# A four-layer decoder on one core: new hand-written interleavings of two streams on every engine, and one more request for a function table

## The chip, the cores and the metric

The program runs on one core of a Trainium2 chip. Its engines are TensorE (PE in the profile; PEld is its loading of weights), VectorE (DVE), ScalarE (ACT), GpSimd (POOL) and SyncE (SP, which here only starts DMAs). Each engine runs its own list of instructions strictly in the order in which the program holds them, and waits on semaphores for the others. The metric is the device time of one execution in microseconds (us).

## The reference

Twelve sublayers run over `x` of 8 sequences x 128 tokens x 128 features; each adds its result to `x` and normalises:

```python
x = _layernorm(x + _L0_attn_ref(x, L0_attn_W_qkv, L0_attn_W_out), axis=-1)
x = _layernorm(x + _L0_xattn_ref(x, ctx_1024, ...), axis=-1)
x = _layernorm(x + _L0_ffn_ref(x, L0_ffn_gate_w, ...), axis=-1)   # 8 experts
x = _layernorm(x + _L1_attn_ref(x, ...), axis=-1)                 # linear attention, rotary
x = _layernorm(x + _L1_xattn_ref(x, ctx_1024, ...), axis=-1)
x = _layernorm(x + _L1_ffn_ref(x, ...), axis=-1)                  # 8 experts
x = _layernorm(x + _L2_attn_ref(x, ...), axis=-1)                 # kernel attention + MLP
x = _layernorm(x + _L2_xattn_ref(x, ctx_1024, ctx_1024, ...), axis=-1)
x = _layernorm(x + _L2_ffn_ref(x, ...), axis=-1)                  # 8 experts
x = _layernorm(x + _L3_attn_ref(x, ...), axis=-1)
x = _layernorm(x + _L3_xattn_ref(x, ctx_1024, ctx_1024, ...), axis=-1)
x = _layernorm(x + _L3_ffn_ref(x, ...), axis=-1)                  # quantised by max |x| of all rows
```

The gated stage that the change touches, `L3x`, needs the log of a sigmoid of its forget gate; the kernel gets it from a softplus, as Exp and then Ln on ScalarE:

```python
log_fg = jax.nn.log_sigmoid(fgate_preact[..., 0])
cs = jnp.cumsum(log_fg, axis=-1)
```

## The kernel before

The eight sequences are cut in pairs. Two pairs run at a time, as **stream a** and **stream b**, which use separate buffers and separate halves of PSUM (four banks each, used as a ring); then both streams run again for the other two pairs (two turns). A stream passes through eleven stages: L0a, L0x, L0f, L1a, L1x, L1f, L2a, L2x, L2f, L3a, L3x (the letter is a for self-attention, x for attention to the context, f for experts); a last block computes the quantised layer for all sequences.

The program of an engine is a generator for each stream. Each `yield` in it ends a **step**: a few instructions, with their waits. `take_turns` (line 402) runs the steps of the two generators in the order that `TURN_ORDER` (line 144) writes out for the engine: "a3 b1" is three steps of stream a, then one of b. Within a stream the order never changes; the table only says how the two streams interleave on that engine. Since an engine issues in order, a step of a that waits also holds back the step of b behind it, whether that one is ready or not.

The names used below, by line of the kernel:

- TensorE: `project` (L458) multiplies the attention's output by its output weights; `by_token` (L464) and `by_feature` (L470) make q, k and v; L441 transposes the normalised x; L479 transposes the maxima; L486 lays a mask or maxima into a bank; L488, L492, L507 and L510 make the scores; L525 (L834 in L1x) multiplies by values; L666 is the router's logits, L673 the experts' up and L681 their down product; L715, L719, L726, L731 and L737 belong to L1a; L843 to L1x's output.
- VectorE: L1143, L1136/L1139 and L1147 are the residual sum, its mean and variance, and the normalised x; L1177 spreads heads over a wide tile; L1192 takes the maxima of scores; L1207 divides attention by its sums; L1392 to L1407 are a chain of L1a that turns decay gates into running products.
- ScalarE: L1715/L1716 give the reciprocal root of the variance; L1743 the exponentials of the scores; L1747/L1748 the reciprocal of their sums (as the exponential of a negated log); L1808 the router's exponential; L1818 the Silu of L0f and L2f; L1877/L1878 those of L1x; L1927 the Gelu of L2a. In L3x, L1974 spreads x over four tiles, L1978/L1979 are the softplus, L1995 the decay matrices, and L2003/L2004 a reciprocal root at the end.

ScalarE must load a table before a function that the present one lacks. The kernel asks for one by name: `use(functions)` (L1680, the load itself is at L1683) records the last name and skips the load where it already holds. `exp_ln()` asks for the table with both Exp and Ln. Where the kernel doesn't ask and the table doesn't fit, the compiler puts a load of its own before the instruction; such a load is shown under the instruction's line.

Of the kernel before, what the change touches and what calls it, by code (L numbers as in the profile page):

```python
# [132 lines left out]
def group_words(g):  # L133
# [9 lines left out]

TURN_ORDER = {
# [12 lines left out]
    "dve":  # L157
# [10 lines left out]
    "act":  # L168
# [8 lines left out]
    "pool":  # L177
        "a1 b1 a1 b2 a3 b1 a1 b1 a1 b1 a3 b1 a1 b2 a1 b2 a1 b1 a4 b1 a2 b4 a1 b2 a2 b2 a1 b1 a3 b1 a1 b2 a1 b2 a1 "
        "b2 a2 b2 a1 b1 ",
    "sp":  # L180
        "a3 b6 a18 b12 a23 b26 ",
}


# [5 lines left out]
def _build(nc, ctx, dram, out):  # L190
# [24 lines left out]
    def const(name):  # L215
        a, w = CONST[name]
        return W["con_sts"][:, a:a + w]
# [24 lines left out]
    def nth(eng, name, n=1):  # L242

        counted[eng, name] = counted.get((eng, name), 0) + n
        return S(name), counted[eng, name]
# [104 lines left out]
    class Order:  # L350
# [11 lines left out]
        def link(self, ins, sem=None):  # L362
            done = self.count(ins, sem)
            self.eng.wait_ge(*done)
# [20 lines left out]
    def by_sample(ap):  # L385
        return ap.rearrange("p (u d) -> p u d", u=NS)
# [25 lines left out]
    with nc.Block(name="layers") as block:  # L412
# [1263 lines left out]
        def _(eng):  # L1676
# [3 lines left out]
            def use(functions):  # L1680

                if table[0] != functions:
                    act.preload_act_table_set(functions)  # L1683
                    table[0] = functions

            def exp_ln():
                use(EXP_LN)

            def program(g):
# [5 lines left out]
                def sem(name):  # L1695
                    return S(f"{name}_{g}")

                def told(name, n=1):
                    return nth("act", f"{name}_{g}", n)
# [4 lines left out]
                def bank(*a):  # L1704
                    act.wait_ge(*ring.full((pair, *a)))
                    return ring.bank((pair, *a))

                def free(*a):
                    return ring.free((pair, *a))
# [259 lines left out]
                def L3x():  # L1969
                    gt = s.gates  # L1970
                    exp_ln()
                    act.wait_ge(*ring.freed((pair, "L3a", "xT")))
                    for j in range(4):
                        o.count(act.activation(s.bd_c[:, :, j], by_sample(s.xT[:]), ACT.Identity,  # L1974
                                               scale=const("head16in64")[:, j:j + 1]), sem("L3x_bd") if j == 3 else None)
                    yield
                    act.wait_ge(*told("L3x_absf"))
                    link(act.activation(gt[:, 5], gt[:, 5], ACT.Exp))  # L1978
                    o.count(act.activation(gt[:, 5], gt[:, 5], ACT.Ln, bias=one[0:64]), sem("L3x_softplus"))  # L1979
                    yield  # L1980
                    yield
                    yield
                    exp_ln()
                    b = bank("L3x", "mx")
                    per_head = lambda k: b[:, 64 * k:64 * k + 64].rearrange("p (u h) -> p u h", u=NS)[:, :, 0:HC]
                    o.count(act.activation(s.small[:, :, 32:40], per_head(0), ACT.Exp, scale=-1.0))
                    link(act.copy(s.small[:, :, 40:48], per_head(1)), free("L3x", "mx"))
                    yield
                    for i in (0, 3, 1, 2):
                        exp_ln()  # L1990
                        b = bank("L3x", "D", i)
                        for j in range(4):
                            cols = slice(j * T, j * T + T)
                            h = 40 + 4 * (i % 2) + j
                            o.count(act.activation(s.p[:, i, cols], b[:, cols], ACT.Exp, bias=s.small[:, i // 2, h:h + 1]),  # L1995
                                    free("L3x", "D", i) if j == 3 else None)
                        yield
                    for u in range(NS):
                        keep("L3x", ("oT", u), s.qk[:, u])
                        yield  # L2000
                    exp_ln()
                    act.wait_ge(*told("L3x_var"))
                    link(act.activation(s.small[:, :, 48:56], s.small[:, :, 16:24], ACT.Ln, bias=eps6, scale=1.0 / DC))  # L2003
                    o.count(act.activation(s.small[:, :, 24:32], s.small[:, :, 48:56], ACT.Exp, scale=-0.5), sem("L3x_rstd"))  # L2004
                    yield
                    rstd()
                    yield
                    yield
                    yield
                    keep("L3x", "xT", xT_all[:, pair * NT:(pair + 1) * NT])  # L2010
                    yield
# [408 lines left out]
```

## Time and profile before

| | us |
|---|---|
| median of 3 runs | 1023.44 |
| lowest, highest | 1021.11, 1024.71 |
| span of the profiled execution | 1020.0 |
| TensorE busy in it | 904.2 |
| VectorE, ScalarE, GpSimd busy | 539.7, 450.7, 50.8 |

The span goes from the first to the last instruction of the core; it is 3.44 us under the median of the runs. A window or a line's row in the views gives busy time by engine, and the mean granted clock of TensorE (1.00 is full speed, 0.50 the lower one). In a timeline a row gives the start, the time from there to the end of the group, engine, line, operation, what it writes and reads, and in square brackets how long the engine had been idle before it and what released it.

### The profile page before, as it was taken

The page shows a single profiled execution, that of the slowest core. Times are in us where ns is not written, and L with a number is a line of the kernel's source. Part 1 is how long each engine was busy: PE and PEld are TensorE (multiplying, and loading weights), DVE is VectorE, ACT ScalarE, POOL GpSimd, SP SyncE. Part 2 cuts the span into 40 slices and gives each one's busy share as a digit, 9 for nine tenths or more (in the row PEclk, how much of TensorE's full clock was granted, in tenths as well). Part 3 has the DMA queues.
Part 4 walks back from the last instruction along what each step waited for, and adds up shares of the span by engine and source line. Part 5 has one row for each costly group of instructions (what it writes and reads, how often), then busy time and mean ns, then how long its engine had stood idle before and what let it go on. Part 6 is the DMA issues. An engine that isn't in the chain of part 4 may idle for free. (4 is left out here: it accounts for less than half of the span.)

```text
span 1020.0 us, 22561 instructions
## 1 busy us (share of the span) xinstructions
PE 904.2 (89%) x9368; PEld 700.2 (69%) x9368; DVE 539.7 (53%) x1569; ACT 450.7 (44%) x923; POOL 50.8 (5%) x71
## 2 busy tenths in 40 slices
PE   7689899999989998997987979989998989899772
PEld 5257768778778785666556757867887868686441
DVE  5733565653265575347636853655325547454345
ACT  2044343453454673574255233244465446433442
POOL 2300000010010000001000000001001000000000
PEclk8799989999999998999999999999999999999965
DMA  9100000401000301103000000040000030000000
GB/s 344 40 2 3 1 1 1 166 2 37 2 19 1 141 3 40 43 12 139 2 12 1 2 1 2 2 166 33 6 1 19 1 140 1 2 1 2 2 1 21
DMA packets 6838, 36.12 MB, mean 35 GB/s; under 512 B 721, under 2 KB 4305, under 8 KB 5458
## 3 DMA queue, kind: packets, MB, share of 16 engines
q1 hardware_dynamic: 6738, 34.68, 9.1%
q8 instruction: 76, 1.25, 0.5%
q14 instruction: 24, 0.20, 0.1%
HBM read 34.15 MB, written 0.52 MB: 34 GB/s over the span
## 5 line engine op out<-in xcount | busy, mean ns | idle before, releaser
L673 PE MATMUL bank<-xT,weights_F 128*128 128x256 f32 x832 | 202.9, 386 | 3.1 <-ACT p L1818 2.6
L673 PEld LDWEIGHTS bank<-xT,weights_F 128*128 128x128 f32 x832 | 152.0, 193 | 26.8 <-issue 4.2
L681 PEld LDWEIGHTS bank<-weights_F,p 128*128 128x128 f32 x1088 | 133.4, 191 | 18.8 <-DVE p L1363 7.2
L681 PE MATMUL bank<-weights_F,p 128*128 128x128 f32 x1088 | 141.3, 278 | 3.7 <-DVE p L1363 3.0
L1743 ACT ACTIVATE p<-bank 128x512 f32<-128x512 f32 x160 | 84.5, 601 | 121.0 <-PE bank L492 120.9
L1683 ACT ACT_TABLE_LOAD x76 | 97.5, 1283 | 12.9 <-DMA weights_con<-in_con 5.9
L1347 DVE SCALAR_TENSOR_TENSOR res<-bank,comb,res 128x128 f32<-128x128 f32 x184 | 55.7, 345 | 74.1 <-PE bank L681 71.6
L1184 DVE TENSOR_REDUCE m_wide<-bank 128x4 f32<-128x512 f32 x96 | 60.3, 684 | 43.4 <-PE bank L780 33.5
L1818 ACT ACTIVATE p<-bank 128x512 f32<-128x512 f32 x72 | 42.5, 597 | 91.6 <-PE bank L673 91.2
L1363 DVE TENSOR_TENSOR p<-p,bank 128x512 f32<-128x512 f32 x72 | 49.3, 685 | 47.5 <-PE bank L673 27.3
L1894 ACT ACTIVATE p<-bank 128x512 f32<-128x512 f32 x64 | 36.6, 598 | 51.3 <-PE bank L673 51.2
L492 PEld LDWEIGHTS bank<-mT,weights_con 32*128 32x128 f32 x1280 | 46.4, 194 | 17.4 <-issue 13.5
L492 PE MATMUL bank<-mT,weights_con 32*128 32x128 f32 x1280 | 55.1, 296 | 0.0
L1715 ACT ACTIVATE lnv<-mv,weights_con 128x2 f32<-128x2 f32 x56 | 16.6, 296 | 74.7 <-DVE mv L1139 72.7
L1192 DVE TENSOR_REDUCE mx<-bank 128x4 f32<-128x512 f32 x64 | 40.2, 682 | 16.5 <-PE bank L488 16.4
L2037 POOL TENSOR_TENSOR xb<-x_tok,biases 128x256 f32<-128x256 f32 x24 | 19.3, 806 | 575.1 <-DVE x_tok L1147 561.5
L525 PE MATMUL bank<-p,vz 128*32 128x128 f32 x1280 | 42.7, 280 | 4.5 <-ACT p L1743 4.4
L525 PEld LDWEIGHTS bank<-p,vz 128*32 128x32 f32 x1280 | 35.2, 112 | 11.0 <-issue 8.4
L525 PE MATMUL bank<-p,weights_con 128*32 128x128 f32 x1280 | 41.7, 275 | 0.0
L1207 DVE TENSOR_TENSOR attnT<-bank,res 128x128 f32<-128x128 f32 x32 | 9.3, 289 | 55.7 <-ACT res L1748 55.7
L525 PEld LDWEIGHTS bank<-p,weights_con 128*32 128x32 f32 x1280 | 35.9, 111 | 1.0
L1147 DVE TENSOR_SCALAR x_tok<-res,mv,rstd 128x128 f32<-128x128 f32 x88 | 26.4, 343 | 18.1 <-ACT rstd L1716 17.6
(319 smaller groups left out, 1356.0 us busy)
## 6 DMA issues: line engine op xcount, KB each, us to landing
weights_F<-in_L1f SPq DMA_DIRECT2D x2, 4096.0 KB, 13.8
weights_F<-in_L0f SPq DMA_DIRECT2D x2, 3456.0 KB, 13.4
weights_F<-in_L2f SPq DMA_DIRECT2D x2, 3456.0 KB, 12.1
weights_Y<-in_L1x_kv SPq DMA_DIRECT2D x2, 1024.0 KB, 10.6
weights_Z<-in_L1x SPq DMA_DIRECT2D x2, 1024.0 KB, 12.9
weights_Y<-in_L2a SPq DMA_DIRECT2D x2, 898.0 KB, 4.4
weights_Z<-in_L2x SPq DMA_DIRECT2D x2, 449.0 KB, 3.2
weights_L3m<-in_L3m SPq DMA_DIRECT2D x2, 288.0 KB, 6.1
```

What stands on the lines that cost most here:

```text
L492: return mm(b[:, j * T:j * T + T], const("pick")[rows32(i), j:j + 1].to_broadcast([32, P]), s.mT[rows32(i), u], start=False, stop=last)
L525: m = mm(b[rows32(g_), cols], w, probs(g_, i), start=n == 0 and i == 0 and not (part and floor is not None), stop=n == len(blocks) - 1 and ...
L673: m = mm(b[:, k * NT:(k + 1) * NT], W[weight][:, f:f + P], s.xT[:], start=True, stop=True)
L681: m = mm(b[:, tk(u)], h[:, tk(u)], w, start=k == 0, stop=k == len(chunks) - 1)
L1184: o.count(dve.tensor_reduce(s.m_wide[:, u, 32 * i:32 * i + 4], heads(b[:], 4), X, ALU.max), free(st, "s", u, 0, i))
L1192: o.count(dve.tensor_reduce(s.mx[:, u, blk, 4 * i:4 * i + 4], heads(b[:], 4), X, ALU.max), free(st, "s", u, blk, i))
L1347: dve.scalar_tensor_tensor(r, y, s.comb[:, u, e:e + 1], r if i else s.x_tok[:, u], ALU.mult, ALU.add))
L1363: o.count(dve.tensor_tensor(s.p[:, 2 + e % 3], s.p[:, e % 2], bank(st, "up", e)[:], ALU.mult), free(st, "up", e))
L1683: act.preload_act_table_set(functions)
L1743: o.count(act.activation(s.p[:, first + i], b[:], ACT.Exp, scale=scale), free(st, "t", u, blk, i))
L1818: o.count(act.activation(s.p[:, e % 2], b[:], ACT.Silu), free(st, "gate", e))
L1894: o.count(act.activation(s.p[:, 2 * (e % 3) + half], b[:], ACT.Gelu_apprx_tanh), free("L1f", f"up{half}", e))
```

## The change

All five strings of `TURN_ORDER` are written anew. Both streams still have the same steps; which stage of one stream stands beside which stage of the other is nearly as before, and the streams change places oftener, in shorter runs. One statement is added in ScalarE's part of `L3x`: a call of `exp_ln()` between the four activations of L1974 and the softplus. Line numbers of the changed kernel are 10 higher from the table on, 11 higher behind that call.

```diff
     "pe":
-        "a1 b1 a2 b1 a2 b1 a2 b3 a1 b1 a1 b1 a1 b2 a1 b2 a3 b1 a2 b1 a1 b2 a1 b1 a1 b2 a1 b1 a1 b1 a2 b1 a6 b1 "
...
+        "a1 b1 a2 b1 a2 b1 a1 b1 a1 b2 a3 b3 a1 b1 a1 b1 a1 b1 a1 b1 a2 b1 a1 b2 a1 b1 a1 b2 a1 b1 a3 b1 a4 b1 a6 "
...
@@ -1974,6 +1984,7 @@
                         o.count(act.activation(s.bd_c[:, :, j], by_sample(s.xT[:]), ACT.Identity,
                                                scale=const("head16in64")[:, j:j + 1]), sem("L3x_bd") if j == 3 else None)
                     yield
+                    exp_ln()
                     act.wait_ge(*told("L3x_absf"))
                     link(act.activation(gt[:, 5], gt[:, 5], ACT.Exp))
                     o.count(act.activation(gt[:, 5], gt[:, 5], ACT.Ln, bias=one[0:64]), sem("L3x_softplus"))
```

What the table does is seen in the lists of instructions. **TensorE near the start**, L0a of stream b (L599, L602, L606, L607, and the context's products L470/L464) beside a's entry into L0x. Before:

```order
15 L599 MATMUL bank<-p,weights_con 128x512
16 L441 MATMUL bank<-weights_con,x_tok 128x128 x2
17 L602 MATMUL bank<-p,weights_con 128x384
18 L606 MATMUL bank<-weights_small,qk 128x128
19 L607 MATMUL bank<-weights_L3a,qk 128x128
20 L470 MATMUL bank<-xT,weights_L0x 128x256 x2
21 L464 MATMUL bank<-weights_L0x,xT 128x128 x2
22 L470 MATMUL bank<-ctxT,weights_L0x 128x256
23 L464 MATMUL bank<-weights_L0x,ctxT 128x128 x2
24 L488 MATMUL bank<-wide,qk 128x512 x4
25 L458 MATMUL bank<-weights_L0a,attnT 128x128 x2
```

After:

```order
15 L609 MATMUL bank<-p,weights_con 128x512
16 L451 MATMUL bank<-weights_con,x_tok 128x128 x2
17 L480 MATMUL bank<-xT,weights_L0x 128x256 x2
18 L474 MATMUL bank<-weights_L0x,xT 128x128 x2
19 L498 MATMUL bank<-wide,qk 128x512 x4
20 L612 MATMUL bank<-p,weights_con 128x384
21 L616 MATMUL bank<-weights_small,qk 128x128
22 L617 MATMUL bank<-weights_L3a,qk 128x128
23 L480 MATMUL bank<-ctxT,weights_L0x 128x256
24 L474 MATMUL bank<-weights_L0x,ctxT 128x128 x2
25 L468 MATMUL bank<-weights_L0a,attnT 128x128 x2
```

Stream a's products from its own x and its first scores (L488, now L498) stand ahead of five of b's groups. **TensorE where a is in L1a and b comes out of L0x** (at 121 us of the trace of before; L441, L666 and the first L673 behind L726 are b's). Before:

```order
90 L441 MATMUL bank<-weights_con,x_tok 128x128 x2
91 L715 MATMUL bank<-xT,weights_L1a 32x128 x2
92 L719 MATMUL bank<-weights_L1a,xT 128x256 x2
93 L464 MATMUL bank<-weights_L1a,xT 128x128 x2
94 L458 MATMUL bank<-weights_L0x,attnT 128x128 x2
95 L726 MATMUL bank<-weights_con,wide 128x64
96 L441 MATMUL bank<-weights_con,x_tok 128x128 x2
97 L731 MATMUL bank<-weights_con,wide 128x128 x2
98 L666 MATMUL bank<-weights_small,xT 128x8 x2
99 L737 MATMUL bank<-weights_con,ks 128x128 x2
100 L673 MATMUL bank<-xT,weights_F 128x256 x8
```

After:

```order
90 L451 MATMUL bank<-weights_con,x_tok 128x128 x2
91 L468 MATMUL bank<-weights_L0x,attnT 128x128 x2
92 L725 MATMUL bank<-xT,weights_L1a 32x128 x2
93 L729 MATMUL bank<-weights_L1a,xT 128x256 x2
94 L474 MATMUL bank<-weights_L1a,xT 128x128 x2
95 L451 MATMUL bank<-weights_con,x_tok 128x128 x2
96 L676 MATMUL bank<-weights_small,xT 128x8 x2
97 L683 MATMUL bank<-xT,weights_F 128x256 x4
98 L736 MATMUL bank<-weights_con,wide 128x64
99 L741 MATMUL bank<-weights_con,wide 128x128 x2
100 L683 MATMUL bank<-xT,weights_F 128x256 x4
```

b's transpose, logits and first experts now stand ahead of a's L726 (now L736), and b's L458 ahead of a's L715. **VectorE at the same place**, where b's residual sum, variance and normalised x (L1143, L1136, L1139, L1147) cross a's chain. Before:

```order
96 L1392 TENSOR_TENSOR wide<-bank,weights_con 128x512
97 L1393 TENSOR_TENSOR wide<-bank,weights_con 128x64x4
98 L1394 TENSOR_TENSOR wide<-bank,weights_con 128x64x4
99 L1396 TENSOR_TENSOR wide<-wide 128x512
100 L1397 TENSOR_SCALAR wide<-wide 128x512
101 L1143 TENSOR_TENSOR res<-bank,xb 128x256
102 L1136 BN_STATS stats<-res 128x6 x2
103 L1139 BN_AGGR mv<-stats 128x2 x2
104 L1400 TENSOR_SCALAR wide<-wide 64x128
```

After:

```order
95 L1153 TENSOR_TENSOR res<-bank,xb 128x256
96 L1146 BN_STATS stats<-res 128x6 x2
97 L1149 BN_AGGR mv<-stats 128x2 x2
98 L1157 TENSOR_SCALAR x_tok<-res,mv,rstd 128x128 x2
99 L1402 TENSOR_TENSOR wide<-bank,weights_con 128x512
100 L1403 TENSOR_TENSOR wide<-bank,weights_con 128x64x4
101 L1404 TENSOR_TENSOR wide<-bank,weights_con 128x64x4
102 L1406 TENSOR_TENSOR wide<-wide 128x512
103 L1407 TENSOR_SCALAR wide<-wide 128x512
```

b's four groups are ahead of the whole chain. **ScalarE where a leaves L2a's attention and b is in L1x** (at 285 us; L1747/L1748 are a's, L1877/L1878 b's). Before:

```order
141 L1911 ACTIVATE p<-bank 128x512 x4
142 L1747 ACTIVATE res<-bank,weights_con 128x256
143 L1748 ACTIVATE res<-res 128x256
144 L1877 ACTIVATE p<-bank 128x512
145 L1878 ACTIVATE p<-p 128x512
146 L1877 ACTIVATE p<-bank 128x512
147 L1878 ACTIVATE p<-p 128x512
```

After:

```order
155 L1921 ACTIVATE p<-bank 128x512 x4
156 L1887 ACTIVATE p<-bank 128x512
157 L1888 ACTIVATE p<-p 128x512
158 L1887 ACTIVATE p<-bank 128x512
159 L1888 ACTIVATE p<-p 128x512
160 L1757 ACTIVATE res<-bank,weights_con 128x256
161 L1758 ACTIVATE res<-res 128x256
```

b's four activations are ahead of a's reciprocal. **ScalarE at the softplus of stream a's first turn**, beside b's Silus of L2f. Before:

```order
247 L1818 ACTIVATE p<-bank 128x512
248 L1683 ACT_TABLE_LOAD
249 L1974 ACTIVATE wide<-xT,weights_con 128x2x128 x4
250 L1683 ACT_TABLE_LOAD
251 L1818 ACTIVATE p<-bank 128x512
252 L1978 ACT_TABLE_LOAD
253 L1978 ACTIVATE wide<-wide 64x128
254 L1979 ACT_TABLE_LOAD
255 L1979 ACTIVATE wide<-wide,weights_con 64x128
256 L1818 ACT_TABLE_LOAD
257 L1818 ACTIVATE p<-bank 128x512 x2
258 L1683 ACT_TABLE_LOAD
```

After:

```order
262 L1828 ACTIVATE p<-bank 128x512 x2
263 L1693 ACT_TABLE_LOAD
264 L1984 ACTIVATE wide<-xT,weights_con 128x2x128 x4
265 L1989 ACTIVATE wide<-wide 64x128
266 L1990 ACTIVATE wide<-wide,weights_con 64x128
267 L1693 ACT_TABLE_LOAD
268 L1828 ACTIVATE p<-bank 128x512 x2
269 L1693 ACT_TABLE_LOAD
```

The six loads of that stretch become three. In the whole list the loads go from 80 to 74; on TensorE the rows of the list go from 805 to 826, on VectorE from 975 to 983, on ScalarE from 597 to 625: the same instructions in shorter groups.

## Rows read from the trace of the kernel before

**Rows 1.** The page, part 1: busy time of each engine.
```profile
PE 904.2 (89%) x9368; PEld 700.2 (69%) x9368; DVE 539.7 (53%) x1569; ACT 450.7 (44%) x923; POOL 50.8 (5%) x71
```
**Rows 2.** Windows: start:end, length, busy us and instructions by engine, clock, DMA.
```profile
120.00:140.00 20.00, 14.21 (x109) 10.60 (x102) 13.09 (x47) 6.40 (x15) 0.74 (x1) 0.83 0.00 1
...
600.00:940.00 340.00, 320.10 (x3270) 261.92 (x3270) 172.13 (x495) 149.55 (x287) 12.97 (x15) 0.99 0.07 28
...
1000.00:1020.00 20.00, 2.67 (x12) 1.48 (x12) 11.84 (x48) 6.66 (x16) 0.72 (x1) 0.50 0.10 27
```
**Rows 3.** Waits of TensorE: line, what released it, us in total, times, longest.
```profile
PE bank L441 <- DVE x_tok L1147: 15.5, 10, 7.6
PE bank L726 <- DVE wide L1404: 6.1, 2, 5.0
```
**Rows 4.** Timeline of TensorE near the start.
```profile
16.63 1.40 PE L602 MATMUL bank<-p,weights_con 1*128 1x384 f32 x2
...
18.97 1.91 PE L470 MATMUL bank<-xT,weights_L0x 128*128 128x256 f32 x4
...
27.33 1.86 PE L486 MATMUL bank<-neg_causal_bf,ident_bf 128*128 128x512 bf16 x4 [2.02 <-DVE mx L1192]
29.12 1.83 PE L488 MATMUL bank<-wide,qk 32*128 32x512 f32 x8
...
35.70 1.14 PE L488 MATMUL bank<-wide,qk 32*128 32x512 f32 x8 [1.47 <-DVE mT L1202]
```
**Rows 5.** Timeline of VectorE near the start, and TensorE's clock from 27.2 us.
```profile
24.70 2.49 DVE L1192 TENSOR_REDUCE mx<-bank 128x4 f32<-128x512 f32 x4 [0.73 <-PE bank L488]
...
27.20:30.60 3.40, 3.27 (x12) 0.95 (x12) 1.61 (x7) 0.50 (x2) 0.72 (x1) 0.50 0.57 161
```
**Rows 6.** Timeline of TensorE and VectorE at a's decay chain.
```profile
129.66 0.34 PE L726 MATMUL bank<-weights_con,wide 64*128 64x64 f32 x1 [4.96 <-DVE wide L1404]
...
132.63 5.47 PE L673 MATMUL bank<-xT,weights_F 128*128 128x256 f32 x16
...
123.92 0.69 DVE L1392 TENSOR_TENSOR wide<-bank,weights_con 128x512 f32<-128x512 f32 x1 [1.19 <-PE bank L719]
...
129.10 0.42 DVE L1404 TENSOR_TENSOR_SCAN wide<-wide 64x128 f32<-64x128 f32 x1
```
**Rows 7.** Window of the lower clock behind that wait.
```profile
129.60:136.40 6.80, 6.58 (x20) 5.13 (x21) 3.90 (x14) 3.41 (x7) 0.00 (x0) 0.50 0.01 2
```
**Rows 8.** Timeline of ScalarE, then of TensorE, where b is in L1x.
```profile
285.36 0.47 ACT L1747 ACTIVATE res<-bank,weights_con 128x256 f32<-128x256 f32 x1 [4.36 <-PE bank L908]
...
288.15 0.63 ACT L1878 ACTIVATE p<-p 128x512 f32<-128x512 f32 x1
...
287.12 0.71 PE L458 MATMUL bank<-weights_Y,attnT 128*128 128x128 f32 x4
```
**Rows 9.** Timeline of ScalarE, then of TensorE, at the softplus.
```profile
434.61 1.28 ACT L1978 ACT_TABLE_LOAD   x1
435.91 0.31 ACT L1978 ACTIVATE wide<-wide 64x128 f32<-64x128 f32 x1
...
437.95 1.28 ACT L1818 ACT_TABLE_LOAD   x1
...
439.89 1.84 PE L673 MATMUL bank<-xT,weights_F 128*128 128x256 f32 x4 [2.08 <-ACT p L1818]
```
**Rows 10.** Timeline of ScalarE, then of TensorE, at the end of a's L0x, second turn.
```profile
540.75 0.31 ACT L2003 ACTIVATE small<-small,weights_con 128x16 f32<-128x16 f32 x1 [3.12 <-DVE small L1622]
...
541.64 0.28 ACT L1747 ACTIVATE res<-bank 128x128 f32<-128x128 f32 x1 [0.33 <-PE bank L525]
...
543.82 0.68 PE L458 MATMUL bank<-weights_L0x,attnT 128*128 128x128 f32 x4 [2.24 <-DVE attnT L1207]
```
**Rows 11.** Timeline of TensorE at two smaller places.
```profile
86.43 1.14 PE L507 MATMUL bank<-wide 32*128 32x512 f32 x8 [1.61 <-DVE attnT L1207]
...
201.35 1.14 PE L745 MATMUL bank<-wide,qk 32*128 32x512 f32 x8 [1.30 <-ACT qk L1722]
```

More of the change, by code:

```diff
@@ L145 @@
     "pe":
[11 rows of a table removed]
-    "dve":
[10 rows of a table removed]
-    "act":
[8 rows of a table removed]
[13 rows of a table added]
+    "dve":
[13 rows of a table added]
+    "act":
[12 rows of a table added]
     "pool":
-        "a1 b1 a1 b2 a3 b1 a1 b1 a1 b1 a3 b1 a1 b2 a1 b2 a1 b1 a4 b1 a2 b4 a1 b2 a2 b2 a1 b1 a3 b1 a1 b2 a1 b2 a1 "
-        "b2 a2 b2 a1 b1 ",
+        "a1 b2 a1 b1 a1 b1 a3 b1 a2 b1 a1 b1 a1 b1 a1 b2 a1 b1 a4 b1 a1 b2 a1 b1 a1 b2 a1 b1 a2 b2 a1 b1 a2 b1 a1 "
+        "b2 a1 b1 a1 b2 a2 b1 a1 b3 a1 b1 ",
     "sp":
-        "a3 b6 a18 b12 a23 b26 ",
+        "b2 a3 b1 a1 b3 a1 b1 a5 b2 a2 b2 a2 b1 a2 b2 a2 b1 a1 b1 a1 b1 a3 b1 a1 b1 a2 b2 a1 b1 a4 b1 a1 b1 a1 b7 "
+        "a1 b2 a1 b2 a1 b1 a2 b6 a1 b1 a3 b1 a2 ",
 }
```

65 rows, old and new, of the table TURN_ORDER are left out of this document.

## The prediction, made before the changed kernel ran

> **What bounds the kernel now.** The page's first part comes first: TensorE is busy 904.2 of 1020.0 us, the other engines little over half of it or less [rows 1]. So the time is TensorE's work plus its idle time, 115.8 us, and the change removes no work of TensorE: it can gain only from idle time and from the clock. Next come the windows. In the long middle of the second turn TensorE is busy 320.1 of 340 us, which leaves 19.9 us there to win; from 120 to 140 it is busy only 14.21, at a clock of 0.83; the last 20 us hold 2.67 us of it [rows 2]. That end is the last block, which needs all sequences and which a new order of two streams can't fill. The waits then say who ends the idle time: the largest are TensorE's transposes waiting for a normalised x (15.5 us in 10 waits, 7.6 of it the one before the last block) and L726 behind VectorE's chain (6.1 us in two, 5.0 of it one) [rows 3]. The third thing to see is that idle time is followed by half speed: behind the 4.96 us the clock is 0.50 for 6.8 us [rows 6, 7], and behind the 2.02 us near the start it is 0.50 for 3.4 us [rows 4, 5]. What a gap costs is thus the gap and up to half of such a stretch.
>
> I went through the two lists engine by engine at each place where TensorE stood for over 1 us, and moved the durations of the trace into the new order.
>
> **The start.** Behind x's transpose TensorE did b's L602, L606 and L607 (16.63 to about 18.97), then a's L470 and L464, then b's context products, then a's scores. Now a's products and scores come first. L470 must wait for the copy of xT, so it starts near 17.2 instead of 18.97 [rows 4]; the scores, which need the spread heads from VectorE, start near 21.1 instead of 23.38, and the maxima (L1192) near 21.9 instead of 24.70 [rows 5]. TensorE fills the time with b's groups and reaches L486 without the wait of 2.02. At equal speed that gains little, since two new short waits, of 0.45 and 1.2 us, stand before L470 and the scores: 2.02 - 1.65 = 0.4 us. But the stretch at half speed that began with the wait goes too: eight products of L488 took 1.83 us in it and 1.14 outside [rows 4], so its 3.4 us hold work of 2.1, a gain of 1.3. Sum **-1.7 us**; the bounds are +0.5 (the new waits stay and the clock drops all the same) and -3.3.
>
> **86 us.** L507 waited 1.61 for VectorE [rows 11]; now a's transpose, logits and two groups of experts stand ahead of it. They cover the wait, but themselves wait for x (0.7 to 1.2). Net **-0.6**, between 0 and -1.6. At 201 us the next part of a's scores is placed behind b's L731 and L737 and covers some of the 1.30 [rows 11]; with one like it at 217 us **-0.6**, between 0 and -1.3.
>
> **The decay chain.** L726 waits for L1392 to L1404, which VectorE ran from 123.92 to 129.52 with b's residual sum and variance in it, 4.96 us of TensorE's time [rows 6]. In the new order b's four groups precede the chain, and TensorE has b's transpose, logits and first experts ahead of L726. The chain begins later, by the time of b's groups that now wait for a rstd from ScalarE, and ends near 132.2. But then TensorE has b's three groups done, which before ended at about 136.6 (the sixteen of L673 from 132.63 are two steps, the first of them at half speed) [rows 6, 7]. Left over are L726, L731 and L737, five products, at 0.34 for L726's at half speed 1.7 us: 132.2 + 1.7 = 133.9 against 136.6, **-2.7 us**. ScalarE has b's rstd behind a reciprocal, so a new wait of about 1.9 stands near 121 us; it is in that walk. Queued behind b's L1363 on VectorE is now a's L1413, which then waits for a Silu behind a table load; who waits for it is L745's side of a. Bounds: -1 (this wait falls due) and -4.3 (the wait and the clock both gone).
>
> **285 us, against the change.** ScalarE's reciprocal L1747 ran at 285.36, at once when L908 was done. Now b's four activations are ahead of it; they need L834's banks, which come at 286.2 and 287.2, so they end near 288.8, as before [rows 8]. The reciprocal comes at 288.8 to 289.7, VectorE's division follows, and L458 starts at 290.0 to 290.3 instead of 287.12 [rows 8], with b's L843 queued behind it on TensorE: 2.1 us later than its place before. Some 0.4 comes back a few us on, where a's Gelu was waited for. **+1.7 us**; bounds 0 (others fill it) and +3.0.
>
> **The softplus.** Before, ScalarE loaded five tables between 429.69 and the Silu at 439.24 and a sixth behind it; L1978, L1979 and L1818 each had one from the compiler [rows 9], at 1.28 us. The call of `exp_ln()` makes Exp and Ln share the table of L1974, and the new order puts the softplus right behind it. Three loads go, 3 x 1.28 = 3.85 us of ScalarE. On the path stands only TensorE's wait of 2.08 for that Silu [rows 9]; once it is gone, TensorE is the bound again. With a bit of the half speed behind it I take **-2.2 us**; bounds 0 (another wait takes its place) and -3.8 (the clock stays full as well: 3.4 us at half speed are 1.7). The trace has Exp beginning at 435.91, 20 ns behind the end of a load that takes 1283 ns. The Trainium skill ("ScalarE: Activation LUTs", "What ACT_TABLE_LOAD costs") counts about 1.38 us of drain beside each load, 2.66 us in all; by that three loads would be worth 8.0 us and the forecast 4.1 us lower. Since the trace shows no drain there, it doesn't enter.
>
> **541 us, against the change.** b's L2003 ran at 540.75, and a's L1747 right behind it at 541.64, released by L525 [rows 10]. Now L1747 is first. L2003 waits with it and ends 1.5 us later; b's VectorE chain of five groups follows, and a's division is queued behind it, which releases L458 (543.82) [rows 10]. **+1.5 us**; bounds 0 and +1.5.
>
> The rest: GpSimd and SyncE are 5% busy and a row of DMA issues, and their new orders move no load to a place where TensorE waits; the loads that go in the second turn lie where TensorE is 94% busy [rows 2]. I count them at nothing; were that cover gone, each would be worth its 1.28 us. The last transposes and the last block keep their order, but for short swaps that cancel.
>
> **Sum.** -1.7 - 0.6 - 0.6 - 2.7 + 1.7 - 2.2 + 1.5 = -4.6 us. Span 1020.0 becomes 1015.4; the median of the runs is 3.44 above the span, so 1023.44 becomes **1018.8**. What was not walked is the larger part of the lists, where no wait over 1 us stands. I take it as nothing, give or take 4 us.
>
> **The rivals.** *Gaps only move* (A): TensorE's 19.9 idle us in the second turn are many waits under 2 us; every step that is moved out of one gap leaves one elsewhere. The 600 to 940 window speaks for it, the long single waits at 27, 129 and 439 against it. Time 1022.5. *The table part does nothing* (B): the wait at 439.89 is ended by something else just as late. Then 1018.8 + 2.2 = 1021.0, inside the bound. *A released step behind an unreleased one* (C): the two places at 285 and 541 show the mechanism: ScalarE's in-order queue gets the step that is released later put first, for 1.6 us each. More short runs mean more such pairs. It decides if more than five more exist that fall on TensorE (3.1 + 4.6 = 7.7 us); at six, 6 x 1.6 = 9.6, time 1028.4; at the five, 1026.8. For it speaks that ScalarE and VectorE wait nearly always, so any swap there moves somebody; against it that most swaps stand beside filled slices. *The clock gives more* (D): if the 6.8 us at half speed behind the decay chain go entirely, 3.4 us come on top, in part counted already; with the bounds of the start it is about 3.8 more, time 1015.
>
> **Chances.** Forecast 0.36, D 0.19, A 0.19, B 0.07, C 0.19. A measurement here tells about 0.3% (3.1 us) from no change. Faster by more: forecast and D, 0.55; within it: A and B, 0.26; slower: C, 0.19. The range goes to 1010 (bounds of the start, chain and softplus together are another 4.4 below D's middle) and to 1026 above, short of C's far half; some 0.2 is left out.
>
> **What would show it.** In the profile of the changed kernel: no wait over 1 us before L486 near 26 us, and the clock at 1.00 from 27 to 30; the wait before L726 (now L736) under 2 us, and fewer us at half speed behind 130; near 287 a wait of about 3 us before L458 (now L468); three loads between L1984 and the Silus and no wait of 2 us near 438; near 542 a wait of 3 to 4 us instead of 2.24. TensorE's busy time should fall by a few us with the clock. I am wrong if waits for ScalarE or VectorE in the second turn grow by over 5 us in sum, or if the half-speed stretches come back at new places.

## The result: half a per cent slower, and where the trace shows it

| | before | changed |
|---|---|---|
| median of 7 runs, us | 1022.41 | 1027.61 |
| lowest to highest | 1019.94 to 1024.71 | 1025.76 to 1033.8 |
| ratio (95% interval) | | 1.0051 (1.0032 to 1.0071) |
| span of the profiled execution | 1020.0 | 1031.8 |

The forecast was 1018.8 us in a range up to 1026.0; the kernel became 0.5% slower. The profiled execution of the changed kernel is the slowest of its seven: the other six have spans from 1023.7 to 1025.8 at clocks of 0.953 to 0.958, this one 1031.8 at 0.942. So the places below are read from it, and the prices from comparisons of many runs.

The page of the changed kernel, part 1 (as [rows 1] of before):

```profile
PE 911.5 (88%) x9368; PEld 712.2 (69%) x9368; DVE 540.5 (52%) x1569; ACT 441.3 (43%) x917; POOL 49.6 (5%) x71
```

TensorE idles 1031.8 - 911.5 = 120.3 us, against 115.8 [rows 1], and is busy 7.3 us longer with the same 9368 products: that is the clock (0.942 against 0.952 in the profiled execution of before). ScalarE has six instructions less, the table loads. Windows of the changed kernel (columns as in [rows 2]):

```profile
120.00:140.00 20.00, 17.52 (x166) 13.56 (x158) 14.27 (x53) 9.95 (x20) 0.73 (x1) 0.83 0.01 2
...
280.00:300.00 20.00, 14.29 (x138) 13.32 (x135) 8.95 (x27) 4.86 (x12) 2.89 (x2) 0.75 0.08 24
350.00:370.00 20.00, 16.33 (x109) 13.87 (x108) 10.84 (x36) 8.22 (x15) 0.00 (x0) 0.83 0.00 0
540.00:560.00 20.00, 14.68 (x230) 10.31 (x228) 11.96 (x44) 7.55 (x26) 1.01 (x3) 0.82 0.01 2
760.00:800.00 40.00, 31.65 (x313) 26.35 (x314) 17.05 (x57) 16.17 (x35) 4.61 (x5) 0.91 0.04 13
```

The same windows of the kernel before, those not in [rows 2]:

```profile
280.00:300.00 20.00, 17.12 (x188) 15.15 (x186) 12.33 (x35) 9.75 (x20) 2.96 (x2) 1.00 0.07 24
350.00:370.00 20.00, 19.45 (x143) 17.13 (x143) 11.11 (x40) 16.19 (x24) 0.73 (x1) 1.00 0.00 1
540.00:560.00 20.00, 15.57 (x135) 12.51 (x124) 13.31 (x59) 10.67 (x26) 1.01 (x3) 0.91 0.00 1
760.00:800.00 40.00, 36.71 (x318) 31.39 (x314) 23.01 (x76) 24.44 (x46) 3.68 (x3) 1.00 0.05 13
```

From 120 to 140 TensorE does 166 products where it did 109, as the forecast has it. But from 280 to 300, from 350 to 370 and from 760 to 800 it is busy less and at a lower clock: 0.75, 0.83 and 0.91 where before all three were at 1.00; from 540 to 560 it is 0.82 against 0.91. Lined up by the work that TensorE has done (busy time times clock, an estimate: single entries move by up to 3 us with the way of matching, the four steps named below by about 1), the changed trace is later than that of before by:

| before at (us) | 120 | 170 | 280 | 310 | 350 | 360 | 450 | 540 | 560 | 750 | 790 | 1020 |
|---|---|---|---|---|---|---|---|---|---|---|---|---|
| later by (us) | +1.3 | -3.0 | -2.7 | +5.4 | +4.8 | +10.0 | +4.7 | +7.5 | +12.4 | +8.5 | +16.6 | +11.7 |

The steps up are at 280 to 310 (8), 350 to 360 (5), 540 to 560 (5) and 750 to 790 (8). Of the third and the fourth, some 1.5 us each belong to the execution of before that was profiled: eleven other traces with the old order near 541 us take 32.3 to 33.0 us from an L525 at 538 to an L673 at 569, it takes 30.9; and near 782 us it does the sixteen products of L931 at full speed, where most others don't (last section). The first and the last are the same place of the program in the two turns: stream a leaves L2a's attention, b is in L1x. TensorE there, in the changed kernel, first and second turn:

```profile
287.37 1.20 PE L468 MATMUL bank<-weights_Y,attnT 128*128 128x128 f32 x4 [3.06 <-DVE attnT L1527]
288.36 6.19 PE L853 MATMUL bank<-weights_Z,p 128*128 128x128 f32 x32
297.20 0.66 PE L451 MATMUL bank<-weights_con,x_tok 128*128 128x128 f32 x2 [2.65 <-DVE x_tok L1157]
...
786.84 0.68 PE L468 MATMUL bank<-weights_Y,attnT 128*128 128x128 f32 x4 [3.06 <-DVE attnT L1527]
787.36 3.74 PE L853 MATMUL bank<-weights_Z,p 128*128 128x128 f32 x32
793.74 0.41 PE L451 MATMUL bank<-weights_con,x_tok 128*128 128x128 f32 x2 [2.65 <-DVE x_tok L1157]
```

and ScalarE in the first:

```profile
283.49 0.60 ACT L1887 ACTIVATE p<-bank 128x512 f32<-128x512 f32 x1 [5.15 <-PE bank L844]
...
285.80 0.46 ACT L1757 ACTIVATE res<-bank,weights_con 128x256 f32<-128x256 f32 x1
```

ScalarE stands idle for 5.15 us until b's bank of L844 is filled, and then does four activations of b, while a's reciprocal L1757, whose bank was full at 282.4, waits behind them; before, it ran at once [rows 8]. TensorE waits 3.06 us for what comes of it. The 32 products of L853 then take 6.19 us, most of it at half speed; the twin in the second turn has them at full speed in 3.74.

### The profile page after: what moved, and what is told of

It is laid out like the page before. It is cut to its first block and busy times, and to the rows that moved or that the text cites. A ratio compares the mean times of both kernels' runs of the same rounds, so it can differ in the third digit from the quotient of the medians.

```text
span 1031.8 us, 22551 instructions
## 1 busy us (share of the span) xinstructions
PE 911.5 (88%) x9368; PEld 712.2 (69%) x9368; DVE 540.5 (52%) x1569; ACT 441.3 (43%) x917; POOL 49.6 (5%) x71
## 5 line engine op out<-in xcount | busy, mean ns | idle before, releaser
L683 PE MATMUL bank<-xT,weights_F 128*128 128x256 f32 x832 | 208.7, 393 | 0.6 <-DVE res L1357 0.6
L683 PEld LDWEIGHTS bank<-xT,weights_F 128*128 128x128 f32 x832 | 155.7, 197 | 27.2 <-issue 6.2
L451 PE MATMUL bank<-weights_con,x_tok 128*128 128x128 f32 x88 | 20.1, 314 | 21.9 <-DVE x_tok L1157 21.7
## 6 DMA issues: line engine op xcount, KB each, us to landing
weights_F<-in_L0f SPq DMA_DIRECT2D x2, 3456.0 KB, 12.6
```

Of the source, the lines that this page charges most:

```text
L683: m = mm(b[:, k * NT:(k + 1) * NT], W[weight][:, f:f + P], s.xT[:], start=True, stop=True)
```

## The experiments

Each kernel is the one before or the changed one with the orders exchanged in a stretch, between points where both orders have taken the same steps of either stream. The edits are shown by what moves in an engine's list (rows without their numbers), since the table's own rows tell nothing. The comparisons are ratios to the kernel before.

**e1, the place taken out of the changed kernel**, and **e2, the place alone put into the kernel before**, in both turns. The two don't cut at the same points: e1 has the old orders from 278 to 305 and from 752 to 792 us, on GpSimd too, and e2 the new ones from 284 to 305 and from 769 to 792, on TensorE, VectorE and ScalarE. So e1 also takes out what the new order does at 757 to 767 us, the third part of below. What moves on ScalarE at the place:

```diff
 L1911 ACTIVATE p<-bank 128x512 x4
+L1877 ACTIVATE p<-bank 128x512
+L1878 ACTIVATE p<-p 128x512
+L1877 ACTIVATE p<-bank 128x512
+L1878 ACTIVATE p<-p 128x512
 L1747 ACTIVATE res<-bank,weights_con 128x256
 L1748 ACTIVATE res<-res 128x256
-L1877 ACTIVATE p<-bank 128x512
-L1878 ACTIVATE p<-p 128x512
-L1877 ACTIVATE p<-bank 128x512
-L1878 ACTIVATE p<-p 128x512
```

> The changed kernel with the old orders on all engines in two stretches, 278 to about 305 us and 752 to about 792 us of the trace of before (a in L2a, b in L1x, both turns); SyncE and all else as changed. Place theory: the loss of the change sits there, where the changed trace has waits of 3.06 (L468) and 2.65 us (L451) in each turn, with half speed behind them. Undone, 6 to 8 us come back: ratio to before 0.997 to 1.000, about 1020. Rival, spread theory: the loss is many small waits and the clock; undone, the ratio stays 1.003 to 1.005.

> The kernel before with the new orders only at that place, both turns (284 to 305 and 769 to 792 us). Place theory: 6 to 8 us slower, ratio 1.006 to 1.008, with the same two waits per turn. Spread theory: under 2 us, ratio up to 1.002.

Measured: e1 0.9945 (0.9928 to 0.9961), e2 1.0123 (1.0101 to 1.0144). Without the place the changed kernel is 5.6 us faster than the one before instead of 5.2 slower; the place alone costs the kernel before 12.6 us. The place theory holds, and the price is above what it expected: 10.8 us in the changed kernel (1.0051 to 0.9945, some 2.6 each way). All else of the change is a gain in sum. In the profiled execution of e1 that gain is the clock: TensorE is busy 896.9 of 1014.7 us, so it idles 117.8, 2.0 more than before, and is busy 7.3 less. Over its 12 runs the clock is 0.958, over the 23 of before beside them 0.951.

**e3, only the reciprocal pair** in the kernel before: the rows above on ScalarE, and on VectorE a's division behind b's two products L1465; **e10**, the same in the first turn alone; **e11**, the same in both turns on ScalarE alone.

> The kernel before with only the first half of that place: ScalarE's reciprocal of a (L1747/L1748) behind b's four activations L1877/L1878, and VectorE's division behind b's L1465, both turns; TensorE's order as before. By my forecast's walk 2.1 us later per turn, of which some comes back: +3.4 us over both turns, ratio 1.003, and a wait of 3 us before L458. Rival: the loss comes from the second half (b's transpose ahead of a's L918 on TensorE); then within 1 us of before, ratio 1.000 to 1.001.

> e3 in the first turn only (the place at 285 us, not the one at 770). If each turn pays the same, half of e3: +3.9 to +4.8 us, ratio 1.004 to 1.0047. If the second turn pays most (the clock behind it), ratio 1.002 or less; my forecast's term for this one place was +1.7 (1.0017).

> e3 with ScalarE's exchange alone, VectorE's order as before, both turns. If ScalarE's queue makes the loss: as e3, 1.008 to 1.010. If VectorE's order (division behind two products) makes it: 1.002 or less.

Measured: e3 1.0093 (1.0067 to 1.0118), e10 1.0042 (1.0019 to 1.0065), e11 1.0083 (1.0058 to 1.0107). So each turn pays about the same, 4.3 us for one of them and 9.5 for both, and ScalarE's queue makes it; VectorE's order adds nothing that the intervals tell. TensorE at the place in e10:

```profile
288.30 1.19 PE L458 MATMUL bank<-weights_Y,attnT 128*128 128x128 f32 x4 [3.06 <-DVE attnT L1517]
289.29 6.10 PE L843 MATMUL bank<-weights_Z,p 128*128 128x128 f32 x32
```

Before, L458 had no wait and L843 one of 0.65, and took 3.84. The new wait is 3.06 - 0.65 = 2.4 us more idle, and L843's 32 products take 6.10 instead of 3.84: 2.3 more. The sum, 4.7, is near the 4.3 that the comparison gives.

**e9, only that pair undone** in the changed kernel, **e13, the second part** in the kernel before (b's transpose L441 and logits ahead of a's L918 and L470 on TensorE, with ScalarE and VectorE to match, both turns), and **e14, a third part**, which the new order has in the second turn alone, 757 to 767 us. e14 on TensorE and VectorE:

```diff
-L834 MATMUL bank<-p,weights_con 64x128 x16
 L884 MATMUL bank<-weights_Y,qk 128x512 x2
 L470 MATMUL bank<-qk,weights_Y 128x256 x4
 L897 MATMUL bank<-wide 128x64 x8
+L834 MATMUL bank<-p,weights_con 64x128 x16
...
-L1465 TENSOR_TENSOR p<-bank,p 128x512 x2
-L1507 TENSOR_SCALAR p<-p 128x512
-L1508 SCALAR_TENSOR_TENSOR wide<-bank,p 128x512
...
+L1465 TENSOR_TENSOR p<-bank,p 128x512
+L1507 TENSOR_SCALAR p<-p 128x512
+L1508 SCALAR_TENSOR_TENSOR wide<-bank,p 128x512
+L1465 TENSOR_TENSOR p<-bank,p 128x512
```

> The changed kernel with only the pair undone that e3 put into the kernel before: ScalarE's reciprocal of a again ahead of b's four activations, VectorE's division again ahead of L1465, both turns. e3 cost 0.9%; if that pair is most of the loss, the ratio falls from 1.005 to 0.996-0.998, the rest of e1's gain (0.9945) being the second half of the place (b's transpose L451 ahead of a's L928). Rival, the pair costs only beside the old order: ratio stays 1.003 or more.

> The kernel before with the new order only behind the reciprocal pair, both turns (288 to 305 and 773 to 792 us): b's transpose L441 and its logits ahead of a's L918 and L470 on TensorE, with ScalarE and VectorE to match. If it costs by itself, what e9 kept and e1 gave back (0.8%, less the third part of e14): ratio 1.003 to 1.006, a wait of 2.65 us before L441 in each turn. If it costs only on top of the pair: 1.001 or less, since the 2.65 stand for the 0.46 + 1.8 of before.

> The kernel before with the third part that e1 undid and e9 didn't: at 757 to 767 us in the second turn alone, b's L834 behind a's L884 to L897 on TensorE, b's activations one by one between a's on ScalarE, b's products L1465 between a's L1507/L1508 on VectorE. The changed trace has waits of 1.37 and 0.47 us there before L844. Cost +1.8 us, 1.002, with half speed behind them 1.0035. Rival: nothing, 1.000.

Measured: e9 1.0027 (1.0009 to 1.0045), e13 1.0020 (0.9999 to 1.0040), e14 1.0032 (1.0014 to 1.0050). e14 has in TensorE's timeline:

```profile
770.77 1.09 PE L834 MATMUL bank<-p,vz 128*64 128x128 f32 x16 [1.37 <-DVE p L1465]
772.34 1.09 PE L834 MATMUL bank<-p,vz 128*64 128x128 f32 x16 [0.47 <-DVE p L1465]
774.04 1.08 PE L908 MATMUL bank<-wide 128*32 128x128 f32 x32 [0.61 <-DVE wide L1512]
```

Three waits, 2.45 us, and the comparison says 3.3. The second part costs 2.0, at the edge of what the comparison tells; its wait of 2.65 stands for 0.46 and 1.7 to 1.8 of before. In the changed kernel the pair undone gives back 2.4 us (1.0051 to 1.0027; with some 2.7 each way that is not clear of nothing), the other two parts 8.4 more (1.0027 to 0.9945), while put into the kernel before the pair costs 9.5 and the other two 5.3. The sums, 10.8 and 14.8, agree within their widths, but are shared otherwise. So the pair's price is shown for the old order around it, and for the changed kernel only that of the whole place. Whether the parts overlap (a second wait in a stretch that is at half speed anyway), or the widths of the intervals make the difference (some 2 us each way), these runs don't settle.

**e4, the decay chain alone, e8, the start alone, e6, 541 us alone.**

> The kernel before with the new orders only from 121 to 139 us (b's transpose, logits and experts ahead of a's L726). Forecast: -2.7 us (-1 to -4.3), ratio 0.9974, the wait of 4.96 gone. Rival, gaps only move: later waits of the two streams take it back, ratio 0.999 to 1.001.

> The kernel before with the new order up to 120 us, the old one behind it. Forecast -1.7 - 0.6 = -2.3 us (+0.5 to -4.9), ratio 0.9978. Rival: the two new short waits and a clock that drops all the same give 0 to +2, ratio 1.000 to 1.002, as the changed trace (0 to +1.3 us at 110 us) leaves open.

> The kernel before with the new order at 537 to 545 us alone: a's reciprocal L1747 ahead of b's L2003. Forecast +1.5 us, ratio 1.0015, wait before L458 3.6 instead of 2.24. Rival: the wait only moves from L441 behind it, ratio 1.000.

Measured: e4 1.0005 (0.9988 to 1.0022), e8 1.0014 (0.9988 to 1.0040), e6 1.0017 (1.0001 to 1.0033). e4 and e8 give nothing that can be told from no change, e6 costs what was forecast. TensorE in e4 where the wait of 4.96 was:

```profile
124.05 0.68 PE L458 MATMUL bank<-weights_L0x,attnT 128*128 128x128 f32 x4 [1.22 <-DVE attnT L1207]
...
127.35 0.41 PE L441 MATMUL bank<-weights_con,x_tok 128*128 128x128 f32 x2 [0.77 <-DVE x_tok L1147]
128.26 0.58 PE L666 MATMUL bank<-weights_small,xT 128*128 128x8 f32 x4 [0.51 <-issue]
...
132.43 0.24 PE L726 MATMUL bank<-weights_con,wide 64*128 64x64 f32 x1 [1.76 <-DVE wide L1404]
133.02 0.41 PE L731 MATMUL bank<-weights_con,wide 128*128 128x128 f32 x2 [0.34 <-DVE wide L1407]
...
136.09 1.14 PE L745 MATMUL bank<-wide,qk 32*128 32x512 f32 x8 [0.71 <-ACT qk L1722]
```

The waits of 0.68, 4.96 and 0.16 us have become six of 0.34 to 1.76, 5.31 us in sum against 5.80. The idle time only moved. But the half speed behind it is gone in this execution, and so the stretch is shorter. L525 stands ahead of it and behind it with the same work between; in before and in e4:

```profile
119.36 1.93 PE L525 MATMUL bank<-p,weights_con 128*32 128x128 f32 x64
...
144.75 1.08 PE L525 MATMUL bank<-p,vz 128*32 128x128 f32 x32
```

```profile
120.53 1.93 PE L525 MATMUL bank<-p,weights_con 128*32 128x128 f32 x64
...
143.66 1.08 PE L525 MATMUL bank<-p,vz 128*32 128x128 f32 x32
```

That is 25.39 us before and 23.13 in e4, 2.3 less, near the forecast of 2.7. The other eleven traces with the old order there all have half speed behind the 4.96, and their stretches are within 0.4 us of before's. The runs don't bear the gain out: +0.5 us, at best -1.2, though e4's mean clock is higher too (0.954 against 0.951). Whether it is lost again later, or few executions have it, isn't shown.

At the start, TensorE in e8:

```profile
24.60 1.02 PE L488 MATMUL bank<-neg_causal_bf,ident_bf 128*128 128x512 bf16 x4
...
29.62 0.30 PE L481 MATMUL bank<-weights_con,m_wide 128*128 128x128 f32 x1 [2.93 <-DVE m_wide L1199]
...
37.68 1.86 PE L488 MATMUL bank<-neg_causal_bf,ident_bf 128*128 128x512 bf16 x4 [2.91 <-DVE mx L1194]
```

The products that waited 2.02 us [rows 4] now start at 24.60 without a wait, as walked. The next two waits on VectorE's maxima are 2.93 and 2.91, where before had 0.56, 1.47 and 2.62: from 16 us to L507 the waits are 9.5 us in before and 10.0 in e8. There the idle time moved.

**e7, the softplus stretch with the call, e15, the call alone**, in the kernel before:

```diff
                     yield
+                    exp_ln()
                     act.wait_ge(*told("L3x_absf"))
```

> The kernel before with the new order at 428 to 446 us (softplus right behind L1974) and the added call; three loads fewer there. Forecast -2.2 us (0 to -3.8), ratio 0.998, the wait of 2.08 before L673 gone. Rival, gaps only move: ratio 0.9995 to 1.0005.

> The kernel before with the added call alone, old orders. The loads there go from six to five (Exp and Ln share one): 1.28 us off ScalarE, of which the wait of 2.08 before L673 shrinks to 0.8. Forecast for this part -1.3 us, ratio 0.9987. Rival, the part does nothing: 1.000; then all of e7's gain (0.9969) is the order's.

Measured: e7 0.9969 (0.9951 to 0.9988), e15 0.9967 (0.9950 to 0.9984). ScalarE and TensorE in e15:

```profile
431.12 1.28 ACT L1683 ACT_TABLE_LOAD   x1
432.41 0.31 ACT L1979 ACTIVATE wide<-wide 64x128 f32<-64x128 f32 x1
432.76 0.40 ACT L1980 ACTIVATE wide<-wide,weights_con 64x128 f32<-64x128 f32 x1
433.17 1.28 ACT L1683 ACT_TABLE_LOAD   x1
...
435.12 1.13 PE L673 MATMUL bank<-xT,weights_F 128*128 128x256 f32 x4 [0.80 <-ACT p L1818]
```

One load less, and the wait went from 2.08 to 0.80 us, by just its 1.28. The four products behind it take 1.13 instead of 1.84 [rows 9]: the 3.4 us at half speed behind the wait are gone too. So the one load is worth 3.4 us, and the two further loads that the new order saves there nothing that the intervals (some 1.8 us each way) tell. Where L1974 and the softplus stand together, as in the new order, the call should have nothing to save: in the kernel before they stand so at 518.34 and 519.93, with no load between. No run has the new order there without the call. e15 also shows the price of a load once more: 1.28 us, with Exp 10 ns behind it and no drain.

**e5, a pair that the forecast hadn't walked**, at 353 us: b's reciprocal ahead of a's table load and first Silu, which saves ScalarE two loads:

```diff
 L1808 ACTIVATE small<-small 128x2x8
-L1683 ACT_TABLE_LOAD
-L1818 ACTIVATE p<-bank 128x512
-L1683 ACT_TABLE_LOAD
 L1747 ACTIVATE res<-bank,weights_con 128x256
 L1748 ACTIVATE res<-res 128x256
 L1683 ACT_TABLE_LOAD
-L1818 ACTIVATE p<-bank 128x512 x2
+L1818 ACTIVATE p<-bank 128x512 x3
```

> The kernel before with one pair of steps exchanged on ScalarE and one on VectorE at 353 us: b's reciprocal (L1747/L1748) ahead of a's table load and first Silu (L1818) of L2f, and the product L1363 ahead of the division L1517; two table loads fewer. Pair theory (the step that is released later stands first): a wait of 3.7 us before the down product L681, with half speed behind it +3 to +5 us, ratio 1.003 to 1.005. Rival, loads cost: two loads fewer give 2.6 us, ratio 0.9975 to 1.000.

> e1 (0.9945) with two more pairs undone: b's reciprocal ahead of a's Silu at 353 us and a's reciprocal ahead of b's L2014 at 541 us. By their local costs (2.1 and 0.3 to 1.5 us) 0.991 to 0.993. Rival, the pairs cost nothing in sum (e5 measured 1.0006): 0.9945 as e1.

Measured: e5 1.0006 (0.9975 to 1.0038), e12 0.9937 (0.9914 to 0.9960). Alone, the wait before L681 is 1.80 us (3.67 in the changed kernel) and the stretch 2.1 us longer in the trace, but the comparison doesn't tell its price. e12, with this pair and the one of 541 us undone as well as the place, has a median of 1016.0 us against 1022.21: the fastest kernel of the study, though its interval overlaps e1's, so that nothing is shown of the two pairs. It is faster than both kernels of the case.

## Why the prediction was wrong, point by point

- **285 us** is the step that failed: forecast +1.7; measured 4.3 for the pair alone in one turn (e10), and 10.8 for the whole place in the changed kernel (e1), 9.1 above the term. The forecast was off by 9.8. The direction and the wait of 3 us before L458 were there. Three things were left out of the term. First, the clock: for waits that go away I counted the half speed behind them, at the start and at the softplus, but none for the waits that come; it is 2.3 of the 4.7 us in e10's trace (there at 6.8 us of half speed; with 3.4 us, as in e3, L843 took 5.30 and the clock's share is 1.5). Second, the **twin in the second turn**: the same exchange stands there, with the same 3.06 and 2.65, and a third part that the first turn lacks (3.3, e14). It had no row in my walk, though TensorE stood 1.83 us before L931 there at 781.77, and the walk was to go to every wait over 1 us. Third, the second part, b's transpose ahead of a's L918: its wait of 2.65 before L451 isn't in the forecast (2.0 for both turns, e13, at the edge of what can be told). One place at +1.7 was two at some 5.
- **What was not walked** was said to be nothing, give or take 4 us. It held the pair at 353 us, behind a TensorE that before waited 0.55 us there, and perhaps gains too: e1, which keeps everything but the place, is at -5.6 us, while the parts of it measured singly (start, decay chain, softplus, 353 and 541 us) add up to +1.4 + 0.5 - 3.2 + 0.6 + 1.7 = +1.0. That leaves a gain of about 6.6 us that no run took alone; with the widths of all six comparisons it is 6.6, give or take 5.4, so it is only just clear of nothing. It may lie in stretches that no term named, or in the decay chain, if its 2.3 us are kept there. Where it lies stays open.
- **Start** (-1.7) and **86 us** (-0.6): e8, which has both, shows no gain. The wait of 2.02 before L486 went, and those behind it grew from 0.56, 1.47 and 2.62 to two of 2.9.
- **201 and 217 us** (-0.6): no run took them alone. In the changed trace the wait of 1.30 is 0.74, and near 217 us L468 waits 0.86 where L666 had waited 0.68.
- **Decay chain** (-2.7): the runs of e4 show no gain, its trace 2.3 us, all of it but 0.5 by the clock. For the idle time rival A's mechanism is the right one, it moved. The walk set all of b's work against one wait and didn't follow the small waits within it.
- **Softplus** (-2.2): right in size for the wrong share. Measured -3.2 and -3.4, all of it by one load and the half speed behind the wait.
- **541 us** (+1.5): right, 1.7 (e6), with 3.64 us before L458 instead of 2.24.
- **Rival C** was the right mechanism for the loss, ScalarE's in-order queue with the later-released step first; its price of 1.6 us each was too low at the place (4.3), about right at 541 us (1.7), and not told at 353. It wanted more than five further pairs (by its own sum five do, 8.0 against 7.7). They weren't needed: the place in its two turns outweighed all gains.
- **The drain** that the Trainium skill counts beside a load ("ScalarE: Activation LUTs", "What ACT_TABLE_LOAD costs") stayed out rightly: by that page a load less would take 2.66 us off ScalarE. The measurement differs, and it decides: e15's wait shrank by 1.28.
- **Two slips that changed nothing.** The forecast "4.1 us lower" by the drain goes past the wait of 2.08 that stood on the path (3.8 us with the clock behind it), and fewer loads can't give more than that. And the bounds of start, chain and softplus are 4.8 us below the forecast, 1014.0, not 4.4 below D's 1015.

Without the place the forecast's sum was -4.6 - 1.7 = -6.3 us, and e1 measured -5.6. That agreement is luck: the start's gain wasn't there, the chain's isn't borne out by the runs, and gains that no term named may have made up for them.

## What to carry to other kernels

When two streams share an in-order engine, price a new order by its pairs: for each step that now stands first, ask whether its input comes later than that of the one behind it, in every turn of the loop, and also where nothing waits now. A table load saved (1.28 us) is cheap beside a wait of 3 us on the engine that bounds the kernel. Count the clock on both sides of the sum: a new wait of 3 us was followed by half speed in eight of nine cases here, and a term that counts the clock only for the waits that go is too favourable.

## What the runs showed of the hardware

Whether half speed follows a wait differs between executions with the same wait. With the old order at the place, TensorE waits 1.71 to 1.72 us before L931 in the first turn in thirteen of the traces (L941 in e1 and e12). In seven the sixteen products behind it take 2.02 us, in five 3.45 to 3.62, in one 3.04. First e15, then e7:

```profile
295.67 2.02 PE L931 MATMUL bank<-weights_Z,p 128*128 128x128 f32 x16 [1.72 <-ACT p L1927]
```

```profile
298.86 3.46 PE L931 MATMUL bank<-weights_Z,p 128*128 128x128 f32 x16 [1.71 <-ACT p L1927]
```

In the second turn the same products, behind a wait of 1.83 or 1.84, take 2.02 us in three of the thirteen and 2.84 to 3.65 in ten; the profiled execution of before is one of the three:

```profile
781.77 2.02 PE L931 MATMUL bank<-weights_Z,p 128*128 128x128 f32 x16 [1.83 <-ACT p L1927]
```

The stretches at half speed behind these waits are 3.4 or 6.8 us long. In the first turn all five traces with the wait of 3.06 before L458 (changed, e2, e3, e10, e11) have one right behind it; in the second turn e2, e3 and e11 have one, and the changed trace has the wait and L853 at full speed behind it. So one wait of 2 to 3 us costs itself and some chance of 1.7 to 3.4 us more (half of such a stretch, an estimate).

One trace against another tells a few us of difference wrongly. In the twelve traces whose lists are those of before up to 120 us, L507 of 47.06 us starts anywhere from 46.12 (e2) to 53.18 us (e3). Over its seven runs the changed kernel's clock went from 0.942 to 0.958 and its span from 1031.8 to 1023.7. Means over runs do tell: the clock was 0.958 for e1 (12 runs), 0.953 for the changed kernel (7) and 0.948 for e2 (5).
